# An attention stage on one core: the loop over head pairs written out, and its value products issued two key groups at a time

## The chip, the core and the metric

The kernel runs on one core of a Trainium2 chip. The metric is the device time of one execution in microseconds (us), where less is better. The profile and its rows come from one execution taken by the hardware profiler. Its engines are named PE (the tensor engine's matmuls), PEld (its weight loads), DVE (vector), ACT (scalar), POOL (GpSimd) and SP (sync, which here issues DMAs).

## The reference, cut to what matters

Four layers follow each other on a residual stream x of 2048 tokens by 128 channels. Only the first is touched by the change.

```python
x = x + attn_a(layernorm(x), W_K, W_Q, W_V, W_O)   # causal softmax attention, 16 heads of 64
x = x + ffn(layernorm(x), ...)                     # 8 experts, one chosen per token
x = x + attn_b(layernorm(x), ...)                  # linear attention
x = x + ffn(layernorm(x), ...)

# attn_a, per head
scores = where(q_pos >= k_pos, Q @ K.T, -1e10)     # 2048 x 2048, causal
attn = softmax(scores / sqrt(64))
z = attn @ V
out = concat(z over heads) @ W_O.T
```

## The kernel before

**Tiling.** `attention` works on 8 pairs of heads, one after the other. A pair's 2048 query rows are cut into 8 steps j of two row tiles each. With two heads and two row tiles a step has four units u = 4j to 4j+3 (a unit is 128 query rows of one head). A unit's keys are covered in chunks of up to 512 columns; unit u has `chunks(u)` = 1 to 4 of them, so a pair has 80 score chunks.

**The engines' parts.** In what follows S u.c is chunk c of unit u.

- `score` S u.c: PE computes two matmuls (L451, L454, queries split in a high and a low part, and for a unit's last chunk the mask, L453) into the next of a ring of 5 PSUM banks. DVE takes the chunk's maximum (L278, and after a unit's last chunk L281, the negated maximum over the chunks).
- `exp` e u.c: ACT computes the exponentials (L371) into `prob`. Only then is the ring's bank free: S number k waits for the exp of number k - 5.
- `turn` t j.g (head 0) and T j.g (head 1): PE transposes the probabilities of key group g (256 keys by the step's 256 query rows, four 128x128 tiles, three in the last group) into one PSUM bank per head, `turn_ps[h]` (L464). ACT copies head 0's bank to `probT[0]` (L378), DVE copies head 1's to `probT[1]` (L287). The next turn of the same head waits until that copy is done, as it writes the same bank.
- `value` V j.g: PE multiplies the turned tiles by v, for both heads, in 64-column halves of the array (L481, 8 instructions), and accumulates into `z_ps`.
- `leave` j: ACT copies z out. `out` j: PE multiplies by W_O (L489). `add` j: DVE adds the result to x (L306, four instructions). `sums` j: DVE sums and inverts the softmax denominators.
- `project` i (0 to 3 keys, 4 to 7 queries) and `vproject` m: PE makes the next pair's projections (L500, L509). ACT writes their high part (L391, L393), DVE their low part (`low` i, L327, L330). SP copies the queries across partitions by DMA (L220).

**The order.** `issue_order` writes one list of these items for a pair. Each engine goes through the same list and does its own part of each item, first in, first out. While the scores of units 4j+4 to 4j+7 are computed, the turns and values of step j (`back_of(j)`) are spread between them; a `None` in `back_of` is an empty place in the spreading. Step 7's turns and values have no scores beside them: they stand between the next pair's projections, or, in the last pair (`last_order`), alone. In the last pair DVE also computes layer-norm statistics behind each `add` (`stats`, L314 to L318).

**The loop.** PE, ACT, DVE, SP and POOL each run pairs 0 to 6 as a hardware loop (`Fori`) over one body; pair 7 is written out behind it. What depends on the pair is addressed by a register. Projection weights are first copied by POOL into `wk_fix` and `wq_fix` (L244).

PE's order in step 6 (with units 29 to 31) and in step 7 (with the projections; P is `project`):

```
S29.1 S29.2 t6.0 T6.0 S29.3 out5 t6.1 T6.1 S30.0 V6.0 S30.1 t6.2 T6.2 S30.2 V6.1 S30.3 t6.3 T6.3
S31.0 V6.2 S31.1 t6.4 T6.4 V6.3 S31.2 t6.5 S31.3 T6.5 V6.4 t6.6 T6.6 V6.5 V6.6
P0 P1 out6 P2 t7.0 T7.0 t7.1 T7.1 V7.0 P3 t7.2 T7.2 V7.1 t7.3 P4 T7.3 V7.2 t7.4 T7.4 P5 V7.3
t7.5 T7.5 V7.4 P6 t7.6 T7.6 V7.5 t7.7 T7.7 P7 V7.6 V7.7
```

Of the kernel before, what the change touches and what calls it, by code (L numbers as in the profile page):

```python
# [14 lines left out]
P = 128  # L15
BANK = 512
# [30 lines left out]
def attention(nc, shp, keep, x_in, w_k, w_q, w_v, w_o, fetch):  # L47
# [7 lines left out]
    SLOTS = 8  # L55

# [23 lines left out]
    def back_of(j):  # L80
        items = []
        for g in range(j + 1):
            items += [("turn", j, 0, g), ("turn", j, 1, g)]
            if g:
                items += [("value", j, g - 1), None]
        return items + [("value", j, j), None, ("leave", j)]
# [56 lines left out]
    with ExitStack() as ctx:  # L143
# [21 lines left out]
        wq_fix, wk_fix = sb("wq_fix", [D, P]), sb("wk_fix", [D, P])  # L165
# [4 lines left out]
        prob = [[sb(f"prob{k}{i}", [P, T - P * (i < 2)]) for i in range(4)] for k in range(2)]  # L170
# [4 lines left out]
        probT = [[sb(f"probT{h}{k}", [P, BANK]) for k in range(2)] for h in range(2)]  # L175
# [12 lines left out]
        s_wfix = sem("s_wfix")  # L188
# [15 lines left out]
        with nc.Block() as block:  # L204

            @block.sync
            def _(sp):
# [16 lines left out]
                with sp.Fori(0, PAIRS - 1) as pair:  # L224
                    second_copies(pair + 1)

            @block.gpsimd
            def _(pool):
# [11 lines left out]
                pool.wait_ge(s_setcp, N_SET - NC)  # L240

                def projection_weights(pair):
                    for fix, n in ((wk_fix, "k"), (wq_fix, "q")):
                        last = pool.tensor_copy(fix[:, :], wT[n][:, bass.ds(pair, 1), :].rearrange("d a f -> d (a f)"))  # L244
                    last.then_inc(s_wfix, 1)

                projection_weights(0)
                with pool.Fori(0, PAIRS - 1) as pair:
                    pool.wait_ge(s_proj, N_PJ * (pair + 1))
                    projection_weights(pair + 1)  # L250

            @block.vector
            def _(dve):
# [14 lines left out]
                def run(items, pair, made):  # L268
                    for it in items:
# [13 lines left out]
                        elif it[0] == "turn" and it[2] == 1:  # L283
# [3 lines left out]
                            dve.tensor_copy(probT[1][n % 2][:, 0:w], turn_ps[1][:, 0:w]).then_inc(s_probT[1], 1)  # L287
# [47 lines left out]
                with dve.Fori(0, PAIRS - 1) as pair:  # L335
                    run(order, pair, pair + 1)
# [3 lines left out]
            def _(act):  # L340
# [21 lines left out]
                def run(items, pair, made):  # L362
                    for it in items:
# [10 lines left out]
                        elif it[0] == "turn" and it[2] == 0:  # L374
# [3 lines left out]
                            act.activation(probT[0][n % 2][:, 0:w], turn_ps[0][:, 0:w], ACT.Copy).then_inc(s_probT[0], 1)  # L378
# [24 lines left out]
                with act.Fori(0, PAIRS - 1) as pair:  # L403
# [4 lines left out]
            def _(pe):  # L408
# [30 lines left out]
                def run(items, pair, made, first):  # L439
                    for it in items:  # L440
# [26 lines left out]
                        elif it[0] == "value":  # L467
                            _, j, g = it
                            n = first_group[j] + g
                            if j == 0:  # L470
                                pe.wait_ge(s_v, N_V * made)
                            if g == 0:
                                pe.wait_ge(s_acc2, STEPS * pair + j + 1)
                            for h in range(2):
                                pe.wait_ge(s_probT[h], N_GR * pair + n + 2)
# [757 lines left out]
```

## Time and profile before

| | |
|---|---|
| median of 3 runs | 1457.94 us (1456.09 to 1460.14) |
| span of the profiled execution, first to last instruction | 1455.8 us |
| PE busy | 1256.4 us, 86% of the span |
| DVE busy | 963.7 us, 66% |
| ACT busy | 793.8 us, 55% |
| POOL busy | 149.0 us, 10% |
| the 7 pairs of the loop, first score of pair 0 to first score of pair 7 | 36.70 us to 988.60 us |

The attention stage ends near 1115 us, so about three quarters of the span belong to it. A busy time is the union of an engine's instructions; PE's matmuls are pipelined, so the distance from one start to the next says more than the length shown for one.

### The profile page before, as it was taken

How to read it: one execution, taken by the hardware profiler on the slowest of the kernel's cores; microseconds unless marked ns; L12 is line 12 of the kernel's file. 1: busy time of each engine (PE TensorE's matmuls, PEld its weight loads, DVE VectorE, ACT ScalarE, POOL GpSimd, SP SyncE). 2: the span in 40 equal slices, each digit the busy share in tenths (PEclk: the TensorE clock that was granted, in tenths of full speed). 3: DMA queues.
4: the chain of work that ended last, by engine and by line, in shares of the span. 5: the costliest groups of instructions: out<-in, count | busy, mean ns of one | idle time of the engine just before them, and what ended most of it. 6: DMA issues, size and time to landing. Idle time of an engine off the chain costs nothing. (4 is left out here: it accounts for less than half of the span.)

```text
span 1455.8 us, 25494 instructions
## 1 busy us (share of the span) xinstructions
PE 1256.4 (86%) x7936; PEld 866.7 (60%) x7936; DVE 963.7 (66%) x2284; ACT 793.8 (55%) x2146; POOL 149.0 (10%) x190
## 2 busy tenths in 40 slices
PE   5999899989998998999899989999997194886376
PEld 3666666666656665666666666656665193443275
DVE  5776577668756775776577668757774264798344
ACT  6766466656665665666466656666663063232143
POOL 1000000000000000000000000000000443554343
PEclk9999999999999999999999999999998596898588
DMA  4940200020002002000200020001000121000023
GB/s 107 157 101 1 61 1 1 1 60 1 2 15 46 1 1 60 1 1 1 61 1 1 1 60 1 2 15 44 1 1 1 37 62 56 1 0 0 21 59 96
DMA packets 52731, 41.62 MB, mean 29 GB/s; under 512 B 14177, under 2 KB 41442, under 8 KB 52578
## 3 DMA queue, kind: packets, MB, share of 16 engines
q1 hardware_dynamic: 50018, 34.50, 11.0%
q0 software_dynamic: 2560, 5.26, 1.1%
q8 instruction: 74, 1.21, 0.3%
q14 instruction: 79, 0.65, 0.1%
HBM read 13.49 MB, written 9.48 MB: 16 GB/s over the span
## 5 line engine op out<-in xcount | busy, mean ns | idle before, releaser
L278 DVE TENSOR_REDUCE at_cmax<-at_ps 128x1 f32<-128x512 f32 (+3 forms) x576 | 350.3, 620 | 167.9 <-PE at_ps L454 166.4
L371 ACT ACTIVATE at_prob<-at_ps,at_nmax 128x512 f32<-128x512 f32 (+3 forms) x640 | 391.4, 621 | 88.1 <-DVE at_nmax L281 53.7
L464 PE MATMUL at_ps<-ident,at_prob 128*128 128x128 f32 x2176 | 309.0, 276 | 20.8 <-DVE at_probT L287 11.5
L451 PE MATMUL at_ps<-at_k_st,at_q_parts 128*128 128x512 f32 (+3 forms) x640 | 289.3, 452 | 31.2 <-issue 22.8
L464 PEld LDWEIGHTS at_ps<-ident,at_prob 128*128 128x128 f32 x2176 | 251.2, 141 | 94.8 <-issue 25.9
L481 PE MATMUL at_ps<-at_probT,at_v 128*64 128x256 f32 (+1 forms) x2304 | 295.0, 379 | 3.8 <-DVE at_probT L287 3.2
L378 ACT ACTIVATE at_probT<-at_ps 128x512 f32<-128x512 f32 (+1 forms) x288 | 165.2, 573 | 236.5 <-PE at_ps L464 234.9
L454 PE MATMUL at_ps<-at_k_st,at_q_parts 128*128 128x512 f32 (+3 forms) x640 | 258.1, 405 | 0.0
L287 DVE COPY at_probT<-at_ps 128x512 f32<-128x512 f32 (+1 forms) x288 | 189.6, 658 | 69.0 <-PE at_ps L464 66.6
L481 PEld LDWEIGHTS at_ps<-at_probT,at_v 128*64 128x64 f32 x2304 | 141.7, 136 | 129.6 <-issue 51.2
L451 PEld LDWEIGHTS at_ps<-at_k_st,at_q_parts 128*128 128x128 f32 x640 | 125.1, 196 | 111.7 <-ACT at_prob L371 59.3
L454 PEld LDWEIGHTS at_ps<-at_k_st,at_q_parts 128*128 128x128 f32 x640 | 129.4, 202 | 1.5
L371 ACT ACTIVATION_READ_ACCUMULATOR at_prob<-at_ps,at_nmax 128x1 f32 x640 | 130.2, 203 | 0.0
L306 DVE SCALAR_TENSOR_TENSOR x<-at_ps,at_rinv,x 128x128 f32<-128x128 f32 x256 | 77.9, 346 | 21.2 <-PE at_ps L489 18.4
L244 POOL COPY at_wk_fix<-at_wT_k 128x128 f32 (+1 forms) x8 | 2.4, 294 | 835.6 <-PE at_ps L500 822.2
L812 ACT ACTIVATE f_hT<-f_ps,f_wfix 128x128 f32<-128x128 f32 x192 | 54.6, 369 | 34.1 <-PE f_ps L857 28.8
L489 PE MATMUL at_ps<-at_wo_bd,at_zT 128*128 (+1 forms) x256 | 67.1, 384 | 2.0 <-ACT at_zT L382 2.0
L850 PE MATMUL f_ps<-ident,f_xs 128*128 128x128 f32 x48 | 14.2, 296 | 56.6 <-DMA f_xs<-slots_in 56.6
L453 PE MATMUL at_ps<-at_maskb,at_identb 128*128 128x128 bf16 x256 | 62.1, 243 | 0.0
L276 DVE TENSOR_REDUCE at_nmax<-at_ps 128x1 f32<-128x128 f32 (+3 forms) x64 | 30.3, 489 | 47.2 <-PE at_ps L454 46.8
L772 DVE COPY f_wfix<-wall 128x1156 f32 x48 | 37.2, 775 | 28.2 <-issue 27.4
L673 POOL DMA_INDIRECT slots_out<-f_ys,f_back x48 | 48.6, 1012 | 62.0 <-DVE f_ys L782 47.6
(186 smaller groups left out, 1279.3 us busy)
## 6 DMA issues: line engine op xcount, KB each, us to landing
at_q_parts<-at_q_parts SPq DMA_DIRECT2D x64, 256.0 KB, 4.0
f_xs<-slots_in SPq DMA_DIRECT2D x48, 64.5 KB
slots_in<-zeros SPq DMA_DIRECT2D x2, 1536.0 KB, 17.9
wall<-in_L_ffn_w_dram SPq DMA_DIRECT2D x1, 2048.0 KB, 17.5
wall<-in_L_ffn_w_dram SPq DMA_DIRECT2D x4, 512.0 KB, 6.2
f_got<-slots_out SPq DMA_DIRECT2D x8, 256.0 KB, 3.6
out_dram<-x SPq DMA_DIRECT2D x4, 256.0 KB, 2.4
slots_out<-f_ys,f_back POOLq DMA_INDIRECT x48
```

The costliest lines, as they stand in the source:

```text
L278: dve.tensor_reduce(cmax[:, u % SLOTS, c:c + 1], bank, AX.X, ALU.max).then_inc(s_cmax, 1)
L287: dve.tensor_copy(probT[1][n % 2][:, 0:w], turn_ps[1][:, 0:w]).then_inc(s_probT[1], 1)
L306: last = dve.scalar_tensor_tensor(x[:, 2 * j + i, :], o_ps[i][:, h * D:(h + 1) * D], rinv[:, j % 2, 2 * i + h:2 * i + h + 1], x[:, 2 * j + ...
L371: act.activation(prob[j % 2][u % 4][:, c * BANK:c * BANK + w], ring[k % RING][:, 0:w], ACT.Exp, bias=nmax[:, u % SLOTS:u % SLOTS + 1], acc ...
L378: act.activation(probT[0][n % 2][:, 0:w], turn_ps[0][:, 0:w], ACT.Copy).then_inc(s_probT[0], 1)
L451: pe.matmul(bank[:, 0:w], q_hi[h][:, r * P:(r + 1) * P], keys, start=True, stop=False)
L453: pe.matmul(bank[:, w - P:w], identb[:, :], maskb[:, :], start=False, stop=False)
L454: last = pe.matmul(bank[:, 0:w], q_lo[h][:, r * P:(r + 1) * P], keys, start=False, stop=True)
L464: last = pe.transpose(turn_ps[h][:, b * P:(b + 1) * P], prob[j % 2][2 * i + h][:, t * P:(t + 1) * P], ident[:, :])
L481: last = pe.matmul(z_ps[rows, to:to + w], v[:, t, rows], probT[h][n % 2][:, 2 * P * b:2 * P * b + w], start=t == 0, stop=last_tile)
L489: last = pe.matmul(o_ps[i], zT[j % 2][:, i * P:(i + 1) * P], wo_bd[:, bass.ds(pair, 1), :, :].rearrange("f a h d -> f (a h d)"), start=Tru ...
L812: last = act.activation(hT[k][:, f, :], ps[2 + c % 2][:, f * P:(f + 1) * P], ACT.Gelu, bias=wfix[k][:, B1.start + f:B1.start + f + 1])
```

## The change

All five hardware loops over the pairs become Python loops: the body is written out seven times, with constants where registers stood. POOL's copies into `wk_fix` and `wq_fix` go, and the projections read `wT` directly. `back_of` no longer issues a value product behind each turn but one run for two key groups behind every second turn; a step with an odd number of groups ends with a run of one. For this `probT` gets three buffers per head instead of two, and four of the `prob` tiles become 256 columns shorter. The number of matmuls, transposes, copies, exponentials and DMAs stays the same.

```diff
+    TURNED = 3
...
         for g in range(j + 1):
             items += [("turn", j, 0, g), ("turn", j, 1, g)]
-            if g:
-                items += [("value", j, g - 1), None]
-        return items + [("value", j, j), None, ("leave", j)]
+            if g and g % 2 == 0:
+                items += [("value", j, (g - 2, g - 1)), None, None, None]
+        return items + [("value", j, (j,) if j % 2 == 0 else (j - 1, j)), None, ("leave", j)]
...
-        wq_fix, wk_fix = sb("wq_fix", [D, P]), sb("wk_fix", [D, P])
...
-        prob = [[sb(f"prob{k}{i}", [P, T - P * (i < 2)]) for i in range(4)] for k in range(2)]
+        prob = [[sb(f"prob{k}{i}", [P, T - P * (i < 2) - 2 * P * (k == 0)]) for i in range(4)] for k in range(2)]
...
-        probT = [[sb(f"probT{h}{k}", [P, BANK]) for k in range(2)] for h in range(2)]
+        probT = [[sb(f"probT{h}{k}", [P, BANK]) for k in range(TURNED)] for h in range(2)]
...
-                with sp.Fori(0, PAIRS - 1) as pair:
+                for pair in range(PAIRS - 1):
                     second_copies(pair + 1)
...
-                projection_weights(0)
-                with pool.Fori(0, PAIRS - 1) as pair:
-                    pool.wait_ge(s_proj, N_PJ * (pair + 1))
-                    projection_weights(pair + 1)
...
-                            dve.tensor_copy(probT[1][n % 2][:, 0:w], turn_ps[1][:, 0:w]).then_inc(s_probT[1], 1)
+                            dve.tensor_copy(probT[1][n % TURNED][:, 0:w], turn_ps[1][:, 0:w]).then_inc(s_probT[1], 1)
...
-                with dve.Fori(0, PAIRS - 1) as pair:
+                for pair in range(PAIRS - 1):
                     run(order, pair, pair + 1)
...
-                            act.activation(probT[0][n % 2][:, 0:w], turn_ps[0][:, 0:w], ACT.Copy).then_inc(s_probT[0], 1)
+                            act.activation(probT[0][n % TURNED][:, 0:w], turn_ps[0][:, 0:w], ACT.Copy).then_inc(s_probT[0], 1)
...
-                with act.Fori(0, PAIRS - 1) as pair:
+                for pair in range(PAIRS - 1):
                     run(order, pair, pair + 1)
...
                         elif it[0] == "value":
-                            _, j, g = it
-                            n = first_group[j] + g
+                            _, j, run_of = it
                             if j == 0:
                                 pe.wait_ge(s_v, N_V * made)
-                            if g == 0:
+                            if run_of[0] == 0:
                                 pe.wait_ge(s_acc2, STEPS * pair + j + 1)
                             for h in range(2):
-                                pe.wait_ge(s_probT[h], N_GR * pair + n + 2)
+                                pe.wait_ge(s_probT[h], N_GR * pair + first_group[j] + run_of[-1] + 2)
+                            for g in run_of:
+                                n = first_group[j] + g
+                                for h, b in ((0, 0), (1, 0), (1, 1), (0, 1)):
+                                    t = 2 * g + b
...
+                                    last = pe.matmul(z_ps[rows, to:to + w], v[:, t, rows], probT[h][n % TURNED][:, 2 * P * b:2 * P * b + w],
+                                                     start=t == 0, stop=last_tile)
+                            if run_of[-1] == j:
                                 last.then_inc(s_z, 1)
...
-                            pe.matmul(ring[(N_SC + i) % RING][:, :], (wk_fix, wq_fix)[kind][:, :], xnT[:, c * BANK:(c + 1) * BANK],
+                            pe.matmul(ring[(N_SC + i) % RING][:, :], wT["kq"[kind]][:, made, :], xnT[:, c * BANK:(c + 1) * BANK],
...
-                with pe.Fori(0, PAIRS - 1) as pair:
+                for pair in range(PAIRS - 1):
                     run(order, pair, pair + 1, False)
```

PE's order in the same two stretches with the change (V6.01 is the run for groups 0 and 1). The exponentials stand where the spreading puts them: e29.0 now follows t6.2 and T6.2, and e30.0 follows t6.4 and T6.4.

```
S29.1 S29.2 t6.0 T6.0 S29.3 out5 t6.1 T6.1 S30.0 t6.2 T6.2 S30.1 V6.01 S30.2 S30.3 t6.3 T6.3 S31.0
t6.4 T6.4 S31.1 V6.23 S31.2 t6.5 S31.3 T6.5 t6.6 T6.6 V6.45 V6.6
P0 P1 out6 P2 t7.0 T7.0 t7.1 T7.1 t7.2 P3 T7.2 V7.01 P4 t7.3 T7.3 t7.4 T7.4 V7.23 P5 t7.5 T7.5
t7.6 P6 T7.6 V7.45 P7 t7.7 T7.7 V7.67
```

In step 5 the order with the change is

```
... T5.0 t5.1 S26.0 T5.1 S26.1 t5.2 S26.2 T5.2 V5.01 S26.3 S27.0 S27.1 t5.3 S27.2 T5.3 S27.3 t5.4
T5.4 S28.0 V5.23 S28.1 S28.2 S28.3 t5.5 S29.0 T5.5 V5.45 S29.1
```

Counted over a pair's list, PE starts a stretch of value matmuls 34 times before and 19 times with the change.

## Rows read from the trace of the kernel before

**Rows 1.** The page: engines, DMA queues, costliest groups.

```profile
PE 1256.4 (86%) x7936; PEld 866.7 (60%) x7936; DVE 963.7 (66%) x2284; ACT 793.8 (55%) x2146; POOL 149.0 (10%) x190
...
q8 instruction: 74, 1.21, 0.3%
...
L278 DVE TENSOR_REDUCE at_cmax<-at_ps 128x1 f32<-128x512 f32 (+3 forms) x576 | 350.3, 620 | 167.9 <-PE at_ps L454 166.4
...
L244 POOL COPY at_wk_fix<-at_wT_k 128x128 f32 (+1 forms) x8 | 2.4, 294 | 835.6 <-PE at_ps L500 822.2
```

**Rows 2.** PE's waits: who was waited for, total us, times, longest.

```profile
PE at_ps L451 <- issue: 22.8, 6, 4.2
```

**Rows 3.** Windows per pair: length, PE, PEld, DVE, ACT, POOL busy, PEclk, DMA, GB/s.

```profile
36.70:171.58 134.88, 127.20 (x833) 85.63 (x833) 93.94 (x202) 84.88 (x224) 0.53 (x2) 1.00 0.49 85
171.58:309.25 137.67, 130.01 (x833) 87.86 (x833) 93.87 (x202) 85.11 (x224) 0.53 (x2) 0.97 0.07 17
...
856.41:988.60 132.19, 128.46 (x832) 86.77 (x833) 93.87 (x202) 84.29 (x223) 0.00 (x0) 0.99 0.05 12
```

**Rows 4.** Windows over the first 20 score chunks of pairs 0 and 6.

```profile
36.70:54.88 18.18, 17.01 (x114) 12.55 (x115) 14.08 (x38) 12.63 (x42) 0.00 (x0) 1.00 1.23 171
...
856.41:876.05 19.64, 18.49 (x114) 13.74 (x115) 14.01 (x38) 12.63 (x42) 0.00 (x0) 0.91 0.01 4
```

**Rows 5.** Timeline of PE: value runs of 8 and 16 instructions, and score chunks.

```profile
911.16 0.48 PE L451 MATMUL at_ps<-at_k_st,at_q_parts 128*128 128x512 f32 x1
...
911.81 1.08 PE L481 MATMUL at_ps<-at_probT,at_v 128*64 128x256 f32 x8
912.82 0.50 PE L451 MATMUL at_ps<-at_k_st,at_q_parts 128*128 128x512 f32 x1
...
939.30 0.40 PE L451 MATMUL at_ps<-at_k_st,at_q_parts 128*128 128x512 f32 x1
...
939.77 1.03 PE L464 MATMUL at_ps<-ident,at_prob 128*128 128x128 f32 x8
...
982.48 1.74 PE L481 MATMUL at_ps<-at_probT,at_v 128*64 128x256 f32 x16
984.15 1.05 PE L509 MATMUL at_ps<-at_wT_v,at_xnT 128*128 x7
```

**Rows 6.** Timeline of PE, ACT and DVE at t6.1 and T6.1.

```profile
941.98 1.04 PE L464 MATMUL at_ps<-ident,at_prob 128*128 128x128 f32 x8
...
942.62 0.60 ACT L378 ACTIVATE at_probT<-at_ps 128x512 f32<-128x512 f32 x1 [1.06 <-PE at_ps L464]
...
942.25 1.25 DVE L306 SCALAR_TENSOR_TENSOR x<-at_ps,at_rinv,x 128x128 f32<-128x128 f32 x4
943.42 0.68 DVE L287 COPY at_probT<-at_ps 128x512 f32<-128x512 f32 x1
```

**Rows 7.** Timeline of PE from S27.3 to S28.1.

```profile
930.36 0.38 PE L451 MATMUL at_ps<-at_k_st,at_q_parts 128*128 128x256 f32 x1
...
932.79 0.50 PE L451 MATMUL at_ps<-at_k_st,at_q_parts 128*128 128x512 f32 x1 [0.45 <-ACT at_prob L371]
```

**Rows 8.** Timeline of PE and ACT from P6 to t7.7.

```profile
977.78 1.12 PE L500 MATMUL at_ps<-at_xnT,at_wq_fix 128*128 128x512 f32 x2
978.75 1.04 PE L464 MATMUL at_ps<-ident,at_prob 128*128 128x128 f32 x8
...
980.82 0.87 PE L464 MATMUL at_ps<-ident,at_prob 128*128 128x128 f32 x6
...
978.95 1.20 ACT L393 ACTIVATE at_q_parts<-at_ps 64x512 fp32r<-64x512 f32 x2 [1.91 <-PE at_ps L500]
980.17 0.60 ACT L378 ACTIVATE at_probT<-at_ps 128x512 f32<-128x512 f32 x1
```

**Rows 9.** Timeline of DVE and PE in pair 7, step 2.

```profile
1007.73 0.49 DVE L314 BATCH_NORM_STATS2 at_stats<-x 128x6 f32<-128x128 f32 x2
...
1009.78 0.66 PE L464 MATMUL at_ps<-ident,at_prob 128*128 128x128 f32 x4 [0.63 <-DVE at_probT L287]
```

More of the change, by code:

```diff
@@ L239, in _ @@
                 pool.memset(wo_bd[:, :, :, :], 0.0).then_inc(s_const, 1)
[L240 to L245, printed above, removed]
-                projection_weights(0)
-                with pool.Fori(0, PAIRS - 1) as pair:
-                    pool.wait_ge(s_proj, N_PJ * (pair + 1))
-                    projection_weights(pair + 1)
             @block.vector
@@ L467, in run @@
                         elif it[0] == "value":
-                            _, j, g = it
-                            n = first_group[j] + g
+                            _, j, run_of = it
                             if j == 0:
                                 pe.wait_ge(s_v, N_V * made)
-                            if g == 0:
+                            if run_of[0] == 0:
                                 pe.wait_ge(s_acc2, STEPS * pair + j + 1)
                             for h in range(2):
-                                pe.wait_ge(s_probT[h], N_GR * pair + n + 2)
-                            for h, b in ((0, 0), (1, 0), (1, 1), (0, 1)):
-                                t = 2 * g + b
-                                last_tile = t == 2 * j + 1
-                                to, w = (P, P) if last_tile else (0, 2 * P)
-                                rows = slice(DH * h, DH * (h + 1))
-                                last = pe.matmul(z_ps[rows, to:to + w], v[:, t, rows], probT[h][n % 2][:, 2 * P * b:2 * P * b + w],
-                                                 start=t == 0, stop=last_tile)
-                            if g == j:
+                                pe.wait_ge(s_probT[h], N_GR * pair + first_group[j] + run_of[-1] + 2)
[3 more added lines that the diff above has]
+                                    t = 2 * g + b
+                                    last_tile = t == 2 * j + 1
+                                    to, w = (P, P) if last_tile else (0, 2 * P)
+                                    rows = slice(DH * h, DH * (h + 1))
+                                    last = pe.matmul(z_ps[rows, to:to + w], v[:, t, rows], probT[h][n % TURNED][:, 2 * P * b:2 * P * b + w],
+                                                     start=t == 0, stop=last_tile)
+                            if run_of[-1] == j:
                                 last.then_inc(s_z, 1)
@@ L489, in run @@
                                 last = pe.matmul(o_ps[i], zT[j % 2][:, i * P:(i + 1) * P],
-                                                 wo_bd[:, bass.ds(pair, 1), :, :].rearrange("f a h d -> f (a h d)"),
+                                                 wo_bd[:, pair, :, :].rearrange("f h d -> f (h d)"),
                                                  start=True, stop=True)
@@ L495, in run @@
                             kind, c = divmod(i, NC)
-                            if i == 0:
-                                pe.wait_ge(s_wfix, made + 1)
                             if not first or i >= RING:
                                 free_bank(N_SC + i, pair, made)
-                            pe.matmul(ring[(N_SC + i) % RING][:, :], (wk_fix, wq_fix)[kind][:, :], xnT[:, c * BANK:(c + 1) * BANK],
+                            pe.matmul(ring[(N_SC + i) % RING][:, :], wT["kq"[kind]][:, made, :], xnT[:, c * BANK:(c + 1) * BANK],
                                       start=True, stop=True).then_inc(s_proj, 1)
@@ L505, in run @@
                             bank = ring[BANKS[V_FIRST + m]]
-                            wv = wT["v"][:, bass.ds(made, 1), :].rearrange("d a f -> d (a f)")
+                            wv = wT["v"][:, made, :]
                             for b in range(TPC):
```

1 line of the change is left out of this document (removed).

## The prediction

> **What bounds the kernel now.** I read the page first, then PE's waits, then windows cut at the first score of each pair, then the timeline around a value product, a turn and a pair's end. The page shows PE busy 86% of the span against 66% for DVE and 55% for ACT [rows 1]. In the pair windows PE is busy 127 to 130 us of 132 to 138, so the attention stage is as long as PE's list [rows 3]. Two things should be seen in it. First, only one wait of PE is large and has no releaser: 22.8 us before the first score of a pair, 6 times [rows 2]. Second, PE takes so much of a pair only because its list mixes its work: DVE and ACT are busy 94 and 85 us of a pair [rows 3], and while PE does something else they finish what it handed them. What PE reaches next is usually ready.
>
> The change touches only attention; the other three layers keep their 340 us.
>
> **The loop written out.** The 6 waits fall at the 6 taken branches. There is none where the loop is left, between pair 6 and pair 7, although that boundary does the same work on all engines: pair 6 lasts 132.19 us, pair 1 137.67 us [rows 3]. Behind each wait the granted clock of PE is down at the 1.2 GHz level for a few us: pair 6's first 20 chunks have mean clock 0.91 and take 19.64 us, pair 0's, which follow no wait, 18.18 us at 1.00 [rows 4]. So a pair without either costs 132.19 - 1.46 = 130.7 us. As a check, pair 0 is 134.88 us with a wait of mean 22.8 / 6 = 3.8 us at its end: 131.1. The seven pairs now take 988.60 - 36.70 = 951.9 us; at 130.7 to 131.1 they take 915 to 918. **Gain 34 to 37 us; I take 37**, as pair 6 shows the straight boundary directly.
>
> Does straight code cost anything instead? Pair 7 is straight code already, and its PE waits nowhere that pair 6 doesn't, except behind the DVE statistics that only it has (below). The instruction queue moved 74 packets, 1.21 MB [rows 1], 16 KB each. That is one packet per 200 or so of the 15,872 PE instructions executed, so I infer that the loop already fetches its body again in every pass. I cost fetching at nothing; the other bound, a stall at each new block, is a rival.
>
> The Trainium skill ("Runtime: NRT & Kernel Launch", Instruction fetch mechanics) says that instructions are prefetched in sequence and that a taken branch out of the window forces a fetch before execution goes on. By that rule the six waits go as well; the trace agrees, with 6 waits for 6 branches.
>
> POOL's copies take 2.4 us for all eight pairs and POOL idles 835.6 us before them [rows 1]; their result is read a whole pair later, except in the opening. Cost and gain nothing. Shorter `prob` tiles and SP's straight list cost nothing either: the copied queries are in place long before pair 7's first score, which does not wait.
>
> **Value runs merged: the gain.** Take x for a full group's matmuls and e for leaving them. One group in a run lasts 912.82 - 911.81 = 1.01 us. Two groups, the second with half of its columns missing in one of two tiles, last 984.15 - 982.48 = 1.67 us [rows 5]. So x + e = 1.01, 1.75 x + e = 1.67: x = 0.88, e = 0.13. Entering costs too: a score chunk lasts 939.77 - 939.30 = 0.47 us with a score's work behind it, and 911.81 - 911.16 = 0.65 before a value [rows 5]: 0.18. A run less saves 0.31 to 0.34, say 0.33 us. With 34 - 19 = 15 runs less per pair: **5.0 us per pair**, 4.0 of it beside the scores and 1.0 beside the projections.
>
> The Trainium skill ("TensorEngine Tiling (Array Packing)", Key Properties) has the rule that changing the tiling mode drains the TensorE. The rows agree: both edges of the run in 64-column halves cost time. By that rule alone the change wins twice, and the sum would be 37 + 40 = 77 us faster.
>
> **Value runs merged: the cost.** What went between two turns of a head is the value product. It gave the copies 1 us. The third `probT` buffer does not help here, since it is `turn_ps`, one bank per head, that the next turn waits for. I follow the new lists with durations from the rows.
>
> *Turnarounds.* ACT's copy of t6.1 starts 0.64 us after the turn and takes 0.60, so head 0 can turn again after 1.3 us [rows 6]. Head 1 needs at least 0.64 + 0.68, some 1.35 with the wait's end, and more where DVE has other items ahead: T6.1 starts at 942.42 (behind 4 of the 8 transposes from 941.98), its copy waits for the add of 1.25 us and ends at 944.10, 1.68 us later [rows 6]. A reduction is 0.62 [rows 1]. A ring bank comes back 2.43 us after the unit's last chunk starts (S27.3 at 930.36, S28.1 at 932.79, released by ACT) [rows 7]. Turns of 4 tiles last 0.4.
>
> *Step 6.* T6.2 stands 0.4 + 0.5 + 0.4 behind T6.1 and needs 1.7: waits 0.5. S30.1 needs e29.0, which ACT now has behind the copy of t6.2: t6.2 at 4.5 us after S29.1, its copy to 5.8, the exp to 6.5, PE there at 5.8: waits 0.75. T6.4 0.1. S31.1 needs e30.0 behind the copy of t6.4: PE there at 12.3, exp done 13.3: 1.0. T6.6 follows T6.5 by one turn, and two reductions stand before T6.5's copy: 0.95. Sum 3.3, of which 0.5 stood there before: 2.8 more.
>
> *Step 5.* T5.1, whose predecessor's copy is now behind the add: 0.85. S27.1 follows S26.3 and S27.0 directly, with the bank due 2.43 after S26.3: 1.4. S27.3 on e26.2, behind t5.3's copy: 0.75. V5.45 directly behind T5.5, whose copy stands behind four reductions: 1.6. Sum 4.6, less 1.7 of waits that go: 2.9 more.
>
> *Steps 1 to 4* by the same reading: V1.01 0.6, T2.2 0.8, T3.2 0.5, V3.23 0.4, T4.2 0.4, T4.4 0.4, less 0.9 that goes: 2.2 more.
>
> *Step 7 beside projections.* A turn right behind a projection finds ACT busy with the projection's two copies: P6 at 977.78, copies 978.95 to 980.15, t7.6's copy to 980.77, next turn 980.82, that is 2.07 us after t7.6 [rows 8]. Today V7.5 fills this. With the change t7.4 and t7.6 come 0.9 after their predecessor: 1.1 each. V7.67 waits for the copies of t7.7: 1.2. t7.2 0.2. Less 0.4 that comes earlier elsewhere: 3.2 more.
>
> Per pair 2.8 + 2.9 + 2.2 + 3.2 = 11.1 more waiting against 5.0 saved: **+6.1 us**. Seven pairs: +43. Pair 7: 7.9 - 4.0 beside its scores, and in the bare tail four waits (0.2, 0.5, 0.5, 0.9) against three runs less: +1.1. **Together +48 us.**
>
> That such lateness reaches PE one for one is seen in pair 7: its statistics on DVE (0.49 us for the first half of them) put the copy before T2.1 back, and PE idles 0.63 for it [rows 9].
>
> Bounds of this term. Least: every copy starts as soon as its tiles are there (1.3 us for both heads) and the ring never waits; then about 5.5 us of waiting per pair remain, +0.5 each, +4. Most: every copy of head 1 has one reduction of 0.62 more ahead than I followed, so 2.0 to 2.3 us for a turnaround; 15 us per pair, +80. I take 48, as it gives each copy the queue that the new list puts ahead of it.
>
> **Sum.** -37 + 48 = +11 us on the span of 1455.8, so 1467 us; the runs' median stands 2.1 us above that span: 1469, say **1468 us**.
>
> **Rivals.**
>
> *The copies hide (faster).* DVE is busy 94 of 131 us, and a value run of 1.9 us lets it and ACT catch up, so most turns meet an engine without backlog. For it: a copy without backlog ends 1.3 us after its turn began [rows 6]. Against it: bursts of three or four scores now follow each run. It decides where the extra waiting falls under 5.0 + 37 / 8 = 9.6 us per pair; 11.1 is not far above. With 6 to 9: value side +8 to +32, so 1429 to 1453, about 1442. Chance 0.28. What the Trainium skill's rule on mode changes gives alone, 77 us, is the far end of this rival, with no new waiting at all: 1381. The 2.07 us of [rows 8] speak against it, since nothing stands between t7.3 and t7.4 any more; under 0.01.
>
> *Balance.* Waiting of 9 to 10.2 us per pair leaves the time within 4.4 us of now (0.3%, about what a measurement of this kernel can tell from no change). Chance 0.14.
>
> *Straight code stalls on instructions (slower).* 74 packets in the span are about 7 blocks a pair [rows 1]. If each new block cost 0.5 us, 8 pairs add 28 us: 1496. Against it: pair 7 shows none. Chance 0.03.
>
> *More waiting than I followed.* Lateness of ACT feeds DVE and back; 14 us or more per pair: 1490 to 1500. Chance 0.07.
>
> *The loop gain does not come,* as the wait is something else at a pair's start: 37 lost, 1505. Against it: pair 7 does not have it. Under 0.01, counted with the last.
>
> **How the numbers follow.** My forecast, 1463 to 1489, has 0.48. Faster 0.28, within 0.3% 0.14, slower 0.58. The range leaves out the lowest of the faster case and the last two: 1438 to 1487.
>
> **What would show it.** In the profile after: no wait "issue" before L451 and clock 1.00 through the pairs; PE waits at L464 for L287 and L378 grown from small to several us per pair, and new ones at L451 for L371; pair windows of about 137 us each, all alike; L481 in runs of 16; t7.4 and t7.6 each 1 us late behind P4 and P5. Pair windows of 131 or less make me wrong: then the copies were ready.

## The result and the profile after

The changed kernel takes 1481.45 us (median of 4 runs, 1481.34 to 1482.64) against 1458.3 us for the kernel before on the same chip (4 runs): ratio 1.016, 95% interval 1.0145 to 1.0174, so 1.6% slower. The forecast was 1468 us, slower; 1481.45 lies inside the range of 1438 to 1487. The direction was right, the size was not: +23 us against +10.

The profiled execution has a span of 1479.7 us, 23.9 us more than before. The page after, two lines that answer to [rows 1]:

```profile
PE 1224.9 (83%) x7936; PEld 871.5 (59%) x7936; DVE 954.9 (65%) x2284; ACT 794.3 (54%) x2146; POOL 143.5 (10%) x174
...
q8 instruction: 59, 0.97, 0.3%
```

PE has as many instructions as before and is busy 31.5 us less, yet the kernel is longer: PE now waits. The windows after, from the first score of a pair to that of the next, for pairs 0, 1 and 6, then the first 20 score chunks of pairs 0 and 6 (columns as in [rows 3]):

```profile
36.32:174.53 138.21, 124.76 (x832) 87.43 (x833) 92.72 (x202) 84.87 (x224) 0.00 (x0) 1.00 0.48 82
174.53:312.68 138.15, 124.74 (x836) 87.43 (x834) 92.60 (x202) 84.99 (x224) 0.00 (x0) 1.00 0.07 16
...
865.43:1003.58 138.15, 124.75 (x836) 87.43 (x834) 92.61 (x202) 84.99 (x224) 0.00 (x0) 1.00 0.07 16
```

```profile
36.32:54.26 17.94, 16.52 (x115) 12.93 (x115) 13.57 (x38) 13.20 (x43) 0.00 (x0) 1.00 1.21 164
...
865.43:883.35 17.92, 16.52 (x118) 12.93 (x116) 13.46 (x38) 13.31 (x43) 0.00 (x0) 1.00 0.04 8
```

The reader should see three things. All pairs are alike, where before they ranged from 132.19 to 137.67 [rows 3]. The granted clock is 1.00 in them, behind a pair's boundary too, where [rows 4] had 0.91. And PE is busy 124.8 us of 138.2, so 13.4 us of a pair are gaps; pair 0 before had 127.20 of 134.88, so 7.7, about half of it the wait at the pair's end.

PE's waits after (who was waited for, total us, times, longest):

```profile
PE at_ps L452 <- DVE at_probT L275: 26.4, 47, 1.5
PE at_ps L470 <- DVE at_probT L275: 25.3, 33, 1.4
PE at_ps L439 <- ACT at_prob L359: 23.5, 38, 1.1
PE at_ps L452 <- ACT at_probT L366: 22.5, 24, 1.0
PE at_ps L470 <- ACT at_probT L366: 8.0, 7, 1.1
PE at_ps L439 <- issue: 0.2, 1, 0.2
```

The lines are renumbered: L452 is the turn (L464 before), L470 the value run (L481), L439 the score's first matmul (L451), L275 and L366 the copies of the turned tiles on DVE and ACT (L287, L378), L359 the exponential (L371), L487 and L496 the projections. The wait of [rows 2], 22.8 us in 6 pieces with no releaser, is gone. What the profile shows now are 149 waits of 0.7 us in the mean, 105.7 us in all, for the copies and for the exponentials queued behind them.

The timeline after of pair 3 in step 6, on PE, then ACT and DVE (start, length, engine, line; in brackets the idle time ahead and what ended it):

```profile
538.71 0.60 PE L452 MATMUL at_ps<-ident,at_prob 128*128 128x128 f32 x4
...
539.54 0.66 PE L452 MATMUL at_ps<-ident,at_prob 128*128 128x128 f32 x4 [0.23 <-DVE at_probT L275]
...
540.67 0.50 PE L439 MATMUL at_ps<-at_k_st,at_q_parts 128*128 128x512 f32 x1 [0.47 <-ACT at_prob L359]
...
541.33 1.95 PE L470 MATMUL at_ps<-at_probT,at_v 128*64 128x256 f32 x16
...
547.68 0.51 PE L439 MATMUL at_ps<-at_k_st,at_q_parts 128*128 128x512 f32 x1 [0.83 <-ACT at_prob L359]
...
553.56 0.55 PE L452 MATMUL at_ps<-ident,at_prob 128*128 128x128 f32 x3 [0.81 <-DVE at_probT L275]
...
539.35 0.60 ACT L366 ACTIVATE at_probT<-at_ps 128x512 f32<-128x512 f32 x1 [0.75 <-PE at_ps L452]
539.84 0.68 ACT L359 ACTIVATE at_prob<-at_ps,at_nmax 128x512 f32<-128x512 f32 x1
...
537.64 1.25 DVE L294 SCALAR_TENSOR_TENSOR x<-at_ps,at_rinv,x 128x128 f32<-128x128 f32 x4
538.81 0.68 DVE L275 COPY at_probT<-at_ps 128x512 f32<-128x512 f32 x1
```

On PE these are t6.2, T6.2, S30.1, V6.01, S31.1 and T6.6. S29.1 started at 534.12, so S30.1 comes 6.55 us and S31.1 13.56 us after it; the prediction had the exponentials that release them done at 6.5 and 13.3. The mechanism is legible in the last four lines: T6.1's copy stands behind the add and ends at 539.49, and T6.2, behind which nothing is left of the value product, starts at 539.54. ACT takes the copy at 539.35 and only then e29.0, so that S30.1 waits for its ring bank.

The same in step 7, beside the projections:

```profile
567.29 1.13 PE L487 MATMUL at_ps<-at_xnT,at_wT_q 128*128 128x512 f32 x2
568.25 1.04 PE L452 MATMUL at_ps<-ident,at_prob 128*128 128x128 f32 x8
570.32 1.09 PE L452 MATMUL at_ps<-ident,at_prob 128*128 128x128 f32 x8 [1.03 <-ACT at_probT L366]
...
576.25 0.66 PE L452 MATMUL at_ps<-ident,at_prob 128*128 128x128 f32 x4 [1.03 <-ACT at_probT L366]
...
582.94 1.73 PE L470 MATMUL at_ps<-at_probT,at_v 128*64 128x256 f32 x16 [1.15 <-ACT at_probT L366]
...
568.45 1.20 ACT L381 ACTIVATE at_q_parts<-at_ps 64x512 fp32r<-64x512 f32 x2 [2.17 <-PE at_ps L487]
569.67 0.60 ACT L366 ACTIVATE at_probT<-at_ps 128x512 f32<-128x512 f32 x1
```

t7.4 starts 2.07 us after t7.3, as t7.7 did behind t7.6 in [rows 8], since ACT first writes the projection's two halves. t7.4, t7.6 and V7.67 wait 1.03, 1.03 and 1.15 us; forecast were 1.1, 1.1 and 1.2.

### The profile page after: what moved, and what is told of

Same layout as the page of the kernel before. It is cut to its first block and busy times, and to the rows that moved or that the text cites. A ratio compares the mean times of both kernels' runs of the same rounds, so it can differ in the third digit from the quotient of the medians.

```text
span 1479.7 us, 22516 instructions
## 1 busy us (share of the span) xinstructions
PE 1224.9 (83%) x7936; PEld 871.5 (59%) x7936; DVE 954.9 (65%) x2284; ACT 794.3 (54%) x2146; POOL 143.5 (10%) x174
## 5 line engine op out<-in xcount | busy, mean ns | idle before, releaser
L266 DVE TENSOR_REDUCE at_cmax<-at_ps 128x1 f32<-128x512 f32 (+3 forms) x576 | 346.7, 619 | 206.9 <-PE at_ps L442 205.3
L359 ACT ACTIVATE at_prob<-at_ps,at_nmax 128x512 f32<-128x512 f32 (+3 forms) x640 | 392.3, 623 | 99.2 <-DVE at_nmax L269 97.7
L452 PE MATMUL at_ps<-ident,at_prob 128*128 128x128 f32 x2176 | 314.8, 276 | 52.8 <-DVE at_probT L275 26.4
L452 PEld LDWEIGHTS at_ps<-ident,at_prob 128*128 128x128 f32 x2176 | 247.6, 140 | 141.6 <-DVE at_probT L275 62.6
L439 PE MATMUL at_ps<-at_k_st,at_q_parts 128*128 128x512 f32 (+3 forms) x640 | 278.3, 435 | 24.2 <-ACT at_prob L359 23.5
L470 PE MATMUL at_ps<-at_probT,at_v 128*64 128x256 f32 (+1 forms) x2304 | 268.5, 373 | 33.3 <-DVE at_probT L275 25.3
L366 ACT ACTIVATE at_probT<-at_ps 128x512 f32<-128x512 f32 (+1 forms) x288 | 165.4, 574 | 203.2 <-PE at_ps L452 199.8
L442 PE MATMUL at_ps<-at_k_st,at_q_parts 128*128 128x512 f32 (+3 forms) x640 | 251.5, 395 | 0.0
L275 DVE COPY at_probT<-at_ps 128x512 f32<-128x512 f32 (+1 forms) x288 | 188.9, 656 | 76.8 <-PE at_ps L452 74.6
L470 PEld LDWEIGHTS at_ps<-at_probT,at_v 128*64 128x64 f32 x2304 | 157.6, 136 | 132.2 <-issue 55.0
L439 PEld LDWEIGHTS at_ps<-at_k_st,at_q_parts 128*128 128x128 f32 x640 | 121.0, 189 | 78.2 <-ACT at_prob L359 49.1
L359 ACT ACTIVATION_READ_ACCUMULATOR at_prob<-at_ps,at_nmax 128x1 f32 x640 | 130.9, 204 | 0.0
L442 PEld LDWEIGHTS at_ps<-at_k_st,at_q_parts 128*128 128x128 f32 x640 | 124.6, 195 | 1.6
L478 PE MATMUL at_ps<-at_wo_bd,at_zT 128*128 128x256 f32 x256 | 66.3, 381 | 1.0 <-ACT at_zT L370 1.0
L381 ACT ACTIVATE at_q_parts<-at_ps 64x512 fp32r<-64x512 f32 x64 | 37.9, 592 | 52.2 <-PE at_ps L487 51.7
L844 PE MATMUL f_ps<-f_xsT,f_wfix 128*128 128x128 f32 x384 | 54.6, 288 | 0.0
```

Source lines behind the costliest of these rows:

```text
L266: dve.tensor_reduce(cmax[:, u % SLOTS, c:c + 1], bank, AX.X, ALU.max).then_inc(s_cmax, 1)
L275: dve.tensor_copy(probT[1][n % TURNED][:, 0:w], turn_ps[1][:, 0:w]).then_inc(s_probT[1], 1)
L359: act.activation(prob[j % 2][u % 4][:, c * BANK:c * BANK + w], ring[k % RING][:, 0:w], ACT.Exp, bias=nmax[:, u % SLOTS:u % SLOTS + 1], acc ...
L366: act.activation(probT[0][n % TURNED][:, 0:w], turn_ps[0][:, 0:w], ACT.Copy).then_inc(s_probT[0], 1)
L439: pe.matmul(bank[:, 0:w], q_hi[h][:, r * P:(r + 1) * P], keys, start=True, stop=False)
L442: last = pe.matmul(bank[:, 0:w], q_lo[h][:, r * P:(r + 1) * P], keys, start=False, stop=True)
```

## The experiments

All ratios are to the kernel before, run beside it on the same chip. "Distance per pair" is the window from the first score of a pair to the first of the next, of pairs in the middle.

### One part alone, both ways

The theory: the loop written out gains about 37 us and the merged runs lose more, by waiting for copies. The kernel with the loop written out alone, on all five engines:

```diff
-                with pe.Fori(0, PAIRS - 1) as pair:
+                for pair in range(PAIRS - 1):
```

> The kernel before with only its five loops over the pairs written out; value products one group at a time, two turned tiles, POOL's weight copies kept. My theory: every pair lasts 130.6 us, as the 6 waits of 3.8 us at taken branches and the half clock behind them go, so 37 us faster than before, 1421 us. Rival (the loop's gain was over-sized, and that is where the 12 us between forecast and result come from): 20 to 28 us faster, 1430 to 1438, with pairs of 132 to 133 us or new waits without a releaser.

Measured: 1416.81 us, ratio 0.9721 (0.97 to 0.9741). Every pair lasts 130.15 to 130.21 us. The loop's part is -41 us.

The runs alone, in the looped kernel (the new `back_of`, three turned tiles, the shorter `prob` tiles, the value code for a run):

> The kernel before with only the value runs merged and three turned tiles; the loops and POOL's weight copies stay. My theory: the runs cost what the pairs of the changed kernel show against 130.6, 7.55 us per pair and 6.6 in the last, and the six branch waits stay, so 59 us slower than before, 1517 us. Rival (loop written out and merged runs disturb each other): under 45 or over 75 us slower.

Measured: 1522.3 us, ratio 1.044 (1.0415 to 1.0465), +64 us. -41 + 64 = +23: the two parts add up to the change.

The changed kernel, with its value products single again:

```diff
-            if g and g % 2 == 0:
-                items += [("value", j, (g - 2, g - 1)), None, None, None]
-        return items + [("value", j, (j,) if j % 2 == 0 else (j - 1, j)), None, ("leave", j)]
+            if g:
+                items += [("value", j, (g - 1,)), None]
+        return items + [("value", j, (j,)), None, ("leave", j)]
```

> The changed kernel with value products one group at a time again, in the places they had before; loops written out, three turned tiles, weights read directly. My theory: the third tile and the direct weights are worth nothing, so the same 1421 us as with the loops alone written out. Rival (the third turned tile or the shorter buffers cost or gain something): 3 us or more away from that run.

Measured: 1417.45 us, 0.9726 (0.9705 to 0.9747), as with the loop alone. So the third turned tile, the shorter `prob` tiles and the weights read in place are worth nothing that can be measured, and all of the loss is the merging. Its window of pair 1 and PE's waits:

```profile
166.41:296.60 130.19, 126.74 (x836) 85.59 (x834) 93.20 (x202) 84.91 (x224) 0.00 (x0) 1.00 0.08 17
```

```profile
PE at_ps L452 <- DVE at_probT L275: 9.6, 12, 1.5
PE at_ps L452 <- ACT at_probT L366: 8.3, 8, 1.2
PE at_ps L439 <- ACT at_prob L359: 7.1, 16, 0.5
PE at_ps L470 <- DVE at_probT L275: 3.3, 8, 0.4
```

28.3 us of such waits against 105.7 after: 77 us more over eight pairs, less what the 15 starts saved. In the windows of pair 1 the gaps grow from 3.45 to 13.41 us, and PE is busy 2.0 us less (126.74 against 124.74): +8.0 us.

### Whose branch was it

PE's loop alone written out, the other four engines looped:

> The kernel before with PE's loop alone written out; ACT, DVE, SP and POOL keep theirs. Theory A (each engine stands still for some 4 us at its own taken branch; PE's stop now covers those of ACT and DVE, which then appear as PE waits on full score banks): part of the gain, 12 to 35 us faster than before, 1423 to 1446. Theory B (only PE's branch costs, as ACT and DVE are ahead of need at a pair's start): all of it, 1417 us.

Measured: 1457.98 us, 0.9989 (0.9966 to 1.0013): no gain. That met neither theory's number. The wait and the start of pair 1:

```profile
PE at_ps L451 <- ACT at_prob L371: 32.1, 22, 4.2
```

```profile
168.71 0.42 PE L454 MATMUL at_ps<-at_k_st,at_q_parts 128*128 128x384 f32 x1
...
172.50 1.62 DVE L276 TENSOR_REDUCE at_nmax<-at_ps 128x1 f32<-128x128 f32 x5 [5.57 <-issue]
...
172.82 0.37 ACT L371 ACTIVATE at_prob<-at_ps,at_nmax 128x128 f32<-128x128 f32 x1 [4.85 <-DVE at_nmax L276]
...
173.33 0.69 PE L451 MATMUL at_ps<-at_k_st,at_q_parts 128*128 128x384 f32 x1 [4.20 <-ACT at_prob L371]
```

PE issues the five score chunks that the ring holds and then waits 4.20 us, because DVE does nothing for 5.57 us ("issue": it waited for nothing that the profile shows) where its own branch stands. The gap begins at 166.93 us and PE's first score of the pair at 167.09, so nearly all of it is time in which DVE had work. The first sections of pairs 1 to 6 are 6 to 7 us longer than pair 0's. The opposite case is PE looped and the other four straight:

> The kernel before with the loops of ACT, DVE, SP and POOL written out and PE's kept. Writing out PE's alone gained nothing, as ACT then stood still in PE's place. Theory (each engine stands still some 4 us at its own taken branch, and before they did so side by side): nothing gained here either, 1451 to 1458 us, with the waits without a releaser at a pair's first score as before. Rival (ACT's branch is the dear one, and PE's only waits for it): 10 us or more faster.

Measured: 1455.49 us, 0.9976 (0.9961 to 0.9991), and PE's wait of [rows 2] as before:

```profile
PE at_ps L451 <- issue: 23.9, 6, 4.2
```

So PE and the others stop side by side at their own branches. Either stop alone costs nearly all of the 41 us; the gain is there only when both go. (The expectation put the second stop to ACT; the rows above show ACT waiting 4.85 us for DVE.)

The instruction queues bear this out. PE looped, the others straight, then PE straight, the others looped:

```profile
q8 instruction: 74, 1.21, 0.4%
q14 instruction: 39, 0.32, 0.1%
```

```profile
q8 instruction: 60, 0.98, 0.3%
q14 instruction: 79, 0.65, 0.2%
```

Queue 8 thus follows PE's loop and queue 14 the other engines': a looped body is fetched again in every pass, and with more packets than the same work written out. In the kernel before, each of PE's six waits holds one packet of queue 8; the boundary between pairs 6 and 7, where no branch is taken (985.0 to 988.6 us), holds none.

### Where the merging loses

Step 7 single again, the rest merged:

```diff
+            if j == STEPS - 1:
+                items += [("value", j, (g - 1,)), None] if g else []
-            if g and g % 2 == 0:
+            elif g and g % 2 == 0:
```

> The changed kernel with single value products in step 7 alone, the step beside the projections and in the tail; steps 0 to 6 keep their merged runs. My theory: step 7 is a third of the loss, 2.8 us per pair in the first seven and 1.6 in the tail, so 21 us faster than the changed kernel, 1460 us. Rival (the loss comes from the score ring alone, which step 7 does not use): within 5 us of the changed kernel.

Measured: 1459.96 us, 1.001 (0.9999 to 1.0021), 21.5 us less than after. The distance per pair is 135.38, 2.8 less, all of it in step 7. The waits beside the projections are a term of their own and do not move elsewhere: the rival is excluded.

The copies made short: ACT and DVE (its line is shown, ACT's has the same edit) copy 128 columns of each turned bank instead of up to 512. These two kernels leave out part of the probabilities of the value products; PE's work is whole.

```diff
-    dve.tensor_copy(probT[1][n % TURNED][:, 0:w], turn_ps[1][:, 0:w]).then_inc(s_probT[1], 1)
+    dve.tensor_copy(probT[1][n % TURNED][:, 0:P], turn_ps[1][:, 0:P]).then_inc(s_probT[1], 1)
```

With runs of two:

> The changed kernel, with the copies of the turned tiles (ACT and DVE) cut to the first 128 of up to 512 columns; the other columns stay at a memset's zeros, so part of the probabilities is left out of the value product. PE's list is unchanged. Theory (the merged runs lose by copies that the next turn waits for): a copy falls from 0.6 to 0.7 us to 0.3, so a pair falls from 138.2 us to 126 to 131. Rival (they lose by the score ring, the reductions and exponentials, which stay as they are): a pair stays at 134 us or more.

With single value products:

> The same short copies (part of the probabilities left out of the value product) in the kernel with single value products and written-out loops. Theory: few waits for copies are there to lose, so a pair falls from 130.2 us by 2 to 4, to 126 to 128, and the distance to the merged runs shrinks from 8.0 us a pair to under 3, as the 15 mode changes less are worth 5 us. Rival: the distance stays at 6 us or more.

Measured: 1424.56 us with runs (0.9756, 0.9697 to 0.9815) and 1395.33 us single (0.9553, 0.9495 to 0.9611). Per pair 131.35 and 127.50: the distance between merged and single falls from 8.0 to 3.85 us. The single kernel's pair fell as its theory said, the merged one's stayed just above 131, and the distance of 3.85 us lies between the theory's 3 and the rival's 6: half and half. PE's waits, first with runs, then single:

```profile
PE at_ps L442 <- ACT at_prob L362: 17.0, 23, 1.1
PE at_ps L473 <- DVE at_probT L278: 16.4, 33, 1.1
PE at_ps L455 <- ACT at_probT L369: 15.0, 21, 0.7
PE at_ps L455 <- DVE at_probT L278: 9.7, 22, 1.1
PE at_ps L473 <- ACT at_probT L369: 6.5, 7, 0.9
```

```profile
PE at_ps L455 <- DVE at_probT L278: 5.1, 12, 1.1
PE at_ps L455 <- ACT at_probT L369: 5.0, 7, 0.7
PE at_ps L442 <- ACT at_prob L362: 1.3, 8, 0.2
```

The length of the copies, with what it holds up behind them on ACT and DVE, is half of the loss. What stays are waits whose length the copy does not set; the candidates are the 0.64 us from a turn's start to its copy's [rows 6], the reductions ahead of a copy on DVE, and the exponentials for the ring. Cut as in the table below, the merged kernel with short copies is 1.0 us a pair shorter than the single one in steps 1 to 4 (50.29 against 51.29) and 4.8 longer in steps 5 to 7 (70.67 against 65.83): with short copies merging pays in the early steps, and 2.0 us of what stays stand beside the projections.

The same 19 starts, but the empty places dealt out, one behind each pair of turns, instead of three behind a run:

```diff
-            items += [("turn", j, 0, g), ("turn", j, 1, g)]
+            items += [("turn", j, 0, g), ("turn", j, 1, g), None]
             if g and g % 2 == 0:
-                items += [("value", j, (g - 2, g - 1)), None, None, None]
+                items += [("value", j, (g - 2, g - 1)), None]
```

> The changed kernel with the same merged runs, but the three empty places behind each run are dealt out: one behind each pair of turns and one behind the run. 19 starts of value stretches a pair, as in the changed kernel. Theory (what a merged run costs is that two turns of a head come too close and score bursts follow): more is between the turns, so a pair falls from 138.2 to 133 to 136 us, mostly in steps 5 and 6, and 1438 to 1464 us in all. Rival (a run of 1.9 us starves DVE and ACT wherever it stands): within 4 us of the changed kernel's 1481.

Measured: 1451.76 us, 0.996 (0.9945 to 0.9975); 134.3 us per pair. About half of the loss is thus where the turns and runs stand in the list and not the number of starts. This half and that of the short copies may overlap; no kernel has both. The theory had the place wrong: of the 3.8 us a pair 1.9 are won in step 7, 1.2 in steps 1 and 2, and 0.8 in steps 5 and 6 (table below). PE's waits change place:

```profile
PE at_ps L439 <- ACT at_prob L359: 35.9, 56, 1.4
PE at_ps L452 <- ACT at_probT L366: 20.0, 33, 1.0
PE at_ps L470 <- DVE at_probT L275: 15.9, 32, 0.7
PE at_ps L452 <- DVE at_probT L275: 6.7, 14, 1.0
```

Turns wait for DVE's copies 6.7 us instead of 26.4, and scores wait for exponentials 35.9 instead of 23.5.

### A version that beats both

Merged is only the last value product with the one before it, behind the last turn and two score places; all else is single:

```diff
+            if 0 < g < j:
+                items += [("value", j, (g - 1,)), None]
+        return items + [None, None, ("value", j, (j - 1, j) if j else (j,)), None, ("leave", j)]
```

> The kernel with single value products and written-out loops, but each step's last two value groups as one run, after the last turn: 29 starts of value stretches per pair instead of 34, and no turn loses its cover. Theory: 5 starts at 0.33 us save 1.7 us a pair and the end runs wait 0.5 to 1 us more for the last copies, so 0 to 8 us faster than with single products, 1410 to 1417. Rival (a run's copies are late here too): 3 or more us slower.

Measured: 1413.83 us, 0.9678 (0.9619 to 0.9736); 129.70 us per pair, against 130.19 single. By sections (below) it gains in steps 0 to 3 and gives 0.8 us back in step 6, whose last two products stood side by side already, so that no start was saved there. So it was kept in steps 0 to 3 alone:

```diff
+            if g and (j > 3 or g < j):
+                items += [("value", j, (g - 1,)), None]
+        if 0 < j <= 3:
+            return items + [None, None, ("value", j, (j - 1, j)), None, ("leave", j)]
+        return items + [None] * (j == 0) * 2 + [("value", j, (j,)), None, ("leave", j)]
```

> Written-out loops and single value products, the last two groups of steps 1 to 3 as one run with two score places before it (step 0's only product later by the same two places), steps 4 to 7 as with single products. From the steps of the run with all ends merged: 0.6, 0.2, 0.3 and 0.4 us a pair saved in steps 0 to 3 and the 0.9 us that it lost in steps 4 to 6 not paid. Theory: steps add up, so a pair of 128.7 to 129.0 us, 1406 to 1410 us in all. Rival (a step's gain is given back in the next): 1413 us or more.

Measured: 1405.33 us, 0.9648 (0.9635 to 0.9661). That is 3.5% under the kernel before and 5.1% under the changed one (1405.33 / 1481.45 = 0.949). Against single value products it is 1.5 us a pair; 0.6 of it stand in step 0, where nothing is merged and the only product merely stands two score places later; with single products it waits 0.41 us (pair 3), there not at all.

A pair cut at starts of PE's items in the timeline, of score chunks, of P0 and of the first `vproject`, in us (S8.1 is the second chunk of unit 8, and so on; step j's turns and values lie between S4j+4 and S4j+8, so the columns from the first to the eighth are steps 0 to 7):

```
                to S8.1  S12.1  S16.2  S20.2  S25.1  S29.1     P0  vproj   next    sum
before, pair 0     6.27   8.63  11.50  14.10  18.52  21.83  20.16  25.24   8.63  134.88
loop alone         6.17   8.57  11.32  14.07  18.37  21.82  20.16  25.24   4.46  130.18
after              6.17   8.69  11.74  14.46  18.53  23.61  22.44  28.04   4.46  138.14
step 7 single      6.17   8.69  11.74  14.46  18.53  23.61  22.44  25.24   4.46  135.34
places dealt out   6.17   8.12  11.13  14.54  18.43  23.22  22.06  26.18   4.46  134.31
ends merged        5.60   8.36  10.99  13.68  18.42  21.96  20.97  25.24   4.46  129.72
ends, steps 0-3    5.60   8.35  11.00  13.67  18.36  21.83  20.16  25.24   4.46  128.67
```

## Why the prediction came out as it did

**The loop, -37 forecast, -41 measured.** The straight boundary was read rightly from pair 6, and clock and wait went as said. The pair came out at 130.2 instead of 130.7. Of the half microsecond 0.33 stands in two sections (11.50 to 11.32, 18.52 to 18.37) that hold the same items in the same order, with constants where registers stood. It does not come from PE: with PE's loop alone written out the two sections still take 11.48 and 18.53 us, with the other four alone 11.32 and 18.37. In pair 3 nearly all of the difference stands at T2.1 and T4.1, which wait for DVE's copy; which DVE instruction was the slower one was not tried. "The 6 waits fall at the 6 taken branches" was right, but it was told of PE alone: DVE has a stop at its own branch too. The change wrote out all five loops, so the number did not suffer; with PE's loop alone, this reading would have been wrong by the whole 41 us. The Trainium skill ("Runtime: NRT & Kernel Launch", Instruction fetch mechanics) says that a taken branch out of the prefetched window forces a fetch before execution goes on. The two half-looped kernels agree: up to 4.2 us on PE, 5.57 us without work on DVE, and queue 8 has a packet in each of PE's waits. That packet takes about 1.4 us (an estimate: 2.3% of 16 engines in the 3.7 us from 305.5 to 309.2); what fills the rest of a stop no run separates.

**Straight code costs nothing: right.** Queue 8 moved 59 packets instead of 74 [rows 1] and queue 14 39 instead of 79, and PE's only attention wait on "issue" is one of 0.2 us. The inference that the loop fetches its body again in every pass was right as well.

**The saving by fewer starts, 5.0 per pair forecast, 4.2 measured.** In the timelines of the changed kernel and of the one with single value products, a run of one group lasts 1.01 us and a run of two 1.88, so leaving costs 0.15, as forecast (0.13); but entering costs 0.09 us behind most scores (0.56 against 0.47) and 0.18 behind a turn (0.53 against 0.35). With the shortest interval of each kind of item before each kind of next item, pair 3 adds up to 117.7 us single and 113.5 merged, so 0.28 per start. The 0.18 of [rows 5] came from one interval before a value product, 0.09 above the shortest of its kind. The 4.2 us depend on how finely kinds are kept apart: told apart only by whether a value product follows, they give 3.7.

**The waits, 11.1 us more per pair forecast, 12.3 measured.** With the shortest time of each kind of item taken off, 12.4 us of waiting per pair are left with single value products and 24.7 after. The gaps that the profile shows grow by less, 10.0 us (3.45 to 13.41), beside a busy time that falls by 2.0. The two counts give the same +8.0; they differ since a matmul's shown length reaches past the next one's start, so that each of the 13 more waits per pair shows about 0.2 us shorter than PE is late (an estimate).

**The step that failed** is the size of the term "value runs merged". It stands in the sum with +6.1 us per pair and +48 in all; measured were +8.0 per pair and +64 (1481.45 against 1417.45 with single products). The mechanism is the one forecast, and the waits stand at the items that were named, except T3.2, T6.4 and t7.2 (0.5, 0.1 and 0.2 us forecast), which do not wait. By steps, net of the starts saved, forecast against measured from the table:

| | starts less | forecast | measured |
|---|---|---|---|
| steps 1 to 4 | 6 | 2.2 - 2.0 = +0.2 | 0.12 + 0.42 + 0.39 + 0.16 = +1.1 |
| step 5 | 3 | 2.9 - 1.0 = +1.9 | +1.8 |
| step 6 | 3 | 2.8 - 1.0 = +1.8 | +2.3 |
| step 7 | 3 | 3.2 - 1.0 = +2.2 | +2.8 |
| sum | 15 | +6.1 | +8.0 |

The steps that were followed item by item came out within 0.6 us; the four that were done "by the same reading" in one line missed most, 0.9 us of the 1.9. There the waits are 2.9 us by the shortest intervals, where 2.2 were forecast, and the saving is 1.7, where 2.0 were. A reduction was priced at 0.62 us, the mean over four widths in [rows 1]; that of a full chunk takes 0.69 (432 of the 576), which made the waits behind reductions a little too short. The 1.9 us times seven are 13 us.

**Pair 7:** +5.0 forecast (3.9 and 1.1), +6.6 measured (124.0 to 130.55 from its first score to its last `out`).

**Where the 23 us come from.** In the spans: the loop -40.7 in pairs 0 to 6 (951.91 to 911.18), the runs +56.1 there (911.18 to 967.25) and +6.6 in pair 7, +2.4 behind the stage's last `out` (343.19 to 345.54) and -0.4 ahead of the first score: +24.0. The last two are outside the change's items. The stretch behind the last `out` was 342.8 to 346.1 us in the kernels cut this way, without a trend, and I had forecast no difference there. The forecast's error is 4 us too little gained and 16 too little lost: the value term is off by a quarter of what was measured, the loop term by a tenth, and the sum is their small difference. This is why +10 could become +23 with the mechanism in place. That the two errors have opposite signs is luck: with the loop's gain at the 37 us forecast the kernel would have taken 1485 us, 17 above the forecast.

**The rivals.** "The copies hide" and "balance" are excluded by the time: the value side costs 8.0 us per pair, where those asked for at most 4.0 and 5.2. The growth of the waiting alone would decide less well. It is 12.3 us by the shortest intervals, above both rivals, but 10.0 by the gaps in the profile, which lies in the band of "balance", 9 to 10.2; the time is lost all the same since the saving is less than the 5.0 that its band was worked out with. "Straight code stalls" and "the loop gain does not come" are excluded by the loop alone, -41. "More waiting than I followed" asked for 14 us or more and 1490 to 1500; in waiting it went 1.2 of the 2.9 us there, in time 13 of the 22 us. The Trainium skill ("TensorEngine Tiling (Array Packing)", Key Properties) says that a change of tiling mode drains the TensorE. The trace agrees, at 0.15 us to leave and 0.09 to 0.18 us to enter, and 15 such pairs of edges are worth 4.2 us per pair, a third of what the waits cost.

**Argued, not shown:** how the half of the loss that short copies leave is shared out between the 0.64 us ahead of each copy, DVE's queue and the ring of five banks. No kernel here changed the ring or gave a head two turn banks, so those shares stay open.

## What to carry to other kernels

Before work is merged to save starts, ask what it stood between: here each value product of 1 us filled the turnaround of a single PSUM bank (0.64 us, plus 0.60 to 0.68 for the copy, plus DVE's queue), and a third buffer behind that bank is worth nothing (1417.45 us with it, 1416.81 without, both with single products). Merge only where other work fills the same place: behind the last turn and two score places it gains 0.9 us per pair in steps 1 to 3 (33.96 to 33.02 us in the table), while the change's own merging lost 0.9 there and 6.9 in steps 5 to 7. A step's products may also stand later than they did: two score places in step 0 were worth 0.6 us without any merging. Here the hardware loop had to be taken out on all engines to gain anything worth having, and a forecast that is the difference of two large terms needs each of them to the size of the difference.

## What the runs showed of the hardware that was not expected

A taken branch stops more than the engine that paces the kernel: PE stood 3.8 us in the mean and 4.2 at most at its own, DVE 5.57 us at its own, and the stops lie side by side. Removing PE's alone gives nothing, removing all but PE's gives 2 us (near the 0.33 us a pair of the sections with T2.1 and T4.1), and removing all of them 41. ACT's and SP's were not seen by themselves.

In the profiled execution of the kernel with step 7 single the granted clock fell to about half, its 1.2 GHz level, in pair 7; no branch over the pairs is left in this kernel. Its windows ahead of the fall and in it (PE busy 5.49 of 7.00 us, then PEclk 0.57), and the value run of 16 in it:

```profile
990.00:997.00 7.00, 5.49 (x37) 4.32 (x35) 6.58 (x21) 4.35 (x14) 0.00 (x0) 1.00 0.00 1
997.00:1001.00 4.00, 3.75 (x18) 2.70 (x19) 0.59 (x3) 1.93 (x7) 0.00 (x0) 0.57 0.00 0
```

```profile
997.25 2.96 PE L473 MATMUL at_ps<-at_probT,at_v 128*64 128x256 f32 x16 [0.76 <-DVE at_probT L278]
```

The next item starts 2.89 us after this run; two such groups took 1.67 us at the full clock [rows 5]. The dip came behind waits of 0.99 and 0.76 us, and cost about 1.6 us in all, with pair 7's section of step 1 beside the same one after. So scattered waits of up to 1 us stood ahead of a lower clock too, not only one of 4 us; the changed kernel, with as many of them, kept 1.00 in the windows above.
